# GNN and Mamba-2 kernel: weighted features stationary in the second adjacency round, Mamba stages three slots later

## The chip, the cores and the metric

The kernel runs on one core of a Trainium2 chip. The metric is the device time of one execution in microseconds (us). A core has five engines that run side by side and wait for each other by semaphores: TensorE (PE in the rows; its weight loads are PEld), VectorE (DVE), ScalarE (ACT), GpSimd (POOL) and SyncE (SP), which here only issues DMAs.

## The reference, cut to what matters

With N = 4096 rows and F = 128 features, a graph layer is followed by a Mamba-2 layer over the sequence of rows:

```
x = layernorm(x0)
U = softmax(where(adj > 0, leaky_relu(x@a1 + (x@a2).T), -9e15), axis=1)
rowsum = sum(U * 0.5 * U, axis=1)
feat = shrink(U@x, x, rowsum)              # round one over adj
pu = U @ feat                              # round two over adj
h = x0 + mix(feat, pu, rowsum, h0)         # = x1 in the kernel
out = h + mamba2(layernorm(h))             # chunks of 128 rows, state carried on
```

Since the leaky relu has two branches, exp(e) factors on each of them into a row weight times a column weight. So U @ v is two products of 0/1 masks with column-weighted features, `row0 * (maskA @ (w0*v)) + row1 * (maskC @ (w1*v))`, divided by the row's sum.

## The kernel before, in words

There are 32 row tiles of 128 rows (NT). Round one turns the adjacency into one byte per edge, `code` (0: no edge, 1 and 2: the two branches), four row tiles (a supertile, IT = 4) at a time, and multiplies the masks made of it with the features. SP writes ("spills") the codes to DRAM, one row tile of 4096 columns per DRAM row, for round two.

Round two runs in slots, one per row tile. In a slot four blocks of eight column tiles follow each other (NB = 4, JB = 8). Per block ScalarE makes maskA and VectorE maskC (128x1024 each, 4 buffers, made two blocks ahead), and `products` multiplies: per side eight matmuls, each with a 128x128 piece of the mask as the stationary operand and 256 columns of `Y` moving. `Y` holds the column-weighted features in two parts, high and low, which are two halves of a bank of the accumulator (accA or accC, two buffers each). Then ScalarE scales accA (`read_acc`, L1005), and VectorE joins accC, adds the halves and makes x1 (L792, L809, L814).

Between the blocks of slot s the Mamba stages of older tiles are worked off, as a software pipeline of five stages (`ok[0]` to `ok[4]`): x1, statistics and normalisation of tile s-1; projection and convolution of s-2 (VectorE's nine L842); decays and turned inputs of s-3; the chunk's outputs of s-4 (p_g, p_y, p_o); the output of tile s-4 (L805) and its store one slot later. GpSimd makes in each slot: rstd2 (L521, L522, after ln_done), x1b (L525), then `base_of` of the slot's own tile (L490 to L509), the decay matrix (L532), four products (L540 to L546) and rs_ready (L552, L553). All queues are in program order. The order within a slot is written out by hand on every engine. `schedule` writes the first 8 slots and the last 4 plus 5 draining ones out one by one, and puts the 20 between them into a hardware loop of four slots a turn.

On VectorE the slot is: gm (L785), the joined sums (L792), wmix (L799), mask(0), the output (L805, waits for rs_ready), x1 (L809, L814), mask(1), statistics (L827, L852), convolution with the small dt chain and the y sums between, yg (L934), mask(2), L940, L942, mask(3). The masks are L638 on VectorE and L986 on ScalarE.

Of the kernel before, what the change touches and what calls it, by code (L numbers as in the profile page):

```python
# [29 lines left out]
P = 128  # L30
# [6 lines left out]
def gnn_ffn_kernel(nc, x, adj, h0, a, temp, W_in, conv_w, conv_b, dt_bias, A_log, D, norm_w, W_out, W_lin, b_lin, out):  # L37
# [20 lines left out]
    with ExitStack() as ctx:  # L58
# [38 lines left out]
        acc_s = sb("acc_s", [P, 2, 2, XC])  # L97
        ps_sum = sb("ps_sum", [P, 2, 2, XC])
# [18 lines left out]
        class Space:  # L117
# [48 lines left out]
        base = adj_space.take(2, F)  # L166
# [22 lines left out]
        yT = adj_space.take(KB, P)  # L189
        state = code_space.take(2, DI)  # L190
# [3 lines left out]
        sum2 = y_space.take(2 * F)  # L194
# [14 lines left out]
            exp_done out_done zcopy""".split()  # L209
# [15 lines left out]

        def schedule(eng, slot):

            def fixed(s_):
                slot(s_, s_ % SLOTS, s_ < NT, s_ + 1 < NT, [0 <= s_ - d < NT for d in range(1, STAGES + 1)])

            for s_ in range(2 * SLOTS):
                fixed(s_)
            with eng.Fori(0, NT // SLOTS - 3) as u:
                for k in range(SLOTS):
                    slot(u * SLOTS + (k + 2 * SLOTS), k, True, True, [True] * STAGES)
            for s_ in range(NT - SLOTS, NT + STAGES):
                fixed(s_)

# [6 lines left out]
        def _(sp):  # L245
# [83 lines left out]
            def slot(s_, k, now, then, ok):  # L329
                if not isinstance(s_, int) or s_ + SLOTS - 1 < NT:  # L330
                    load_codes(s_ + (SLOTS - 1), (k + SLOTS - 1) % SLOTS)
                if then:
                    load_rows(s_ + 1, (k + 1) % 2)
                if ok[4]:
                    store(s_ - 5, (k - 1) % 2)
# [7 lines left out]
        def _(pool):  # L343
# [141 lines left out]
            def base_of(s_, k):  # L485
# [13 lines left out]
                link(g.tensor_tensor(w, wz, r, ALU.mult))  # L499
                link(g.tensor_tensor(wz, w, zn, ALU.mult))  # L500
# [8 lines left out]
                link(g.tensor_tensor(base[:, k % 2], featw[:, 0], featw[:, 1], ALU.add))  # L509
# [5 lines left out]
            def slot(s_, k, now, then, ok):  # L515
# [10 lines left out]
                if now:  # L526
                    base_of(s_, k)
# [33 lines left out]
        def _(dve):  # L561
# [169 lines left out]
            def mask2(n, k, j):  # L731
# [3 lines left out]
                mask_c(n + R1, code[:, 0, k, b * JB * P:(b + 1) * JB * P], b)  # L735

# [34 lines left out]
            def slot(s_, k, now, then, ok):  # L771
                def mask(j):

                    if (now and not (isinstance(s_, int) and s_ == 0) if j + LEAD < NB else then):
                        mask2(s_ * NB + (j + LEAD), (k + (j + LEAD) // NB) % SLOTS, j + LEAD)
# [3 lines left out]
                part = sum2.rearrange("p (a b) -> p a b", a=2)  # L779
# [6 lines left out]
                if ok[0]:  # L786

                    T = s_ - 1
                    row = v.snap(T) if not isinstance(T, int) else T
# [17 lines left out]
                if ok[0]:  # L807
                    dve.wait_ge(S["vch"], halves)
                    halves = step(v.tensor_tensor(part[:, 0], part[:, 0], part[:, 1], ALU.add))  # L809
                if ok[0]:  # L810

                    dve.wait_ge(S["vch"], halves)
# [552 lines left out]
```

## Time and profile before

| | |
|---|---|
| time, median of 3 runs (lowest, highest) | 981.47 us (979.46, 982.36) |
| span of the profiled execution | 981.8 us; no other time of that execution is given |
| TensorE, VectorE, ScalarE, GpSimd busy | 88%, 79%, 61%, 66% |
| mean granted TensorE clock | 0.926 of 2.4 GHz |
| round one / change of rounds / round two | to about 405 us / about 440 us / to the end |

The profile is one execution. A row of the timeline has the start and the duration in us, the engine, the line, the operation, output and inputs with their shapes, and how many of them are merged; in brackets stands the idle time of the engine before it and who ended it. A row of the groups (`--lines` of the trace) has the busy time in us and the mean duration in ns, then the idle time ahead. A row of the stretches gives for each engine the busy us and the count of instructions in the order PE, PEld, DVE, ACT, POOL, then the granted clock, the DMA engines' busy share and GB/s. Matmuls are pipelined: a single one's duration holds its latency, so the spacing of a run of them says more.

### The profile page before, as it was taken

How to read it: one execution, taken by the hardware profiler on the slowest of the kernel's cores; microseconds unless marked ns; L12 is line 12 of the kernel's file. 1: busy time of each engine (PE TensorE's matmuls, PEld its weight loads, DVE VectorE, ACT ScalarE, POOL GpSimd, SP SyncE). 2: the span in 40 equal slices, each digit the busy share in tenths (PEclk: the TensorE clock that was granted, in tenths of full speed). 3: DMA queues.
4: the chain of work that ended last, by engine and by line, in shares of the span. 5: the costliest groups of instructions: out<-in, count | busy, mean ns of one | idle time of the engine just before them, and what ended most of it. 6: DMA issues, size and time to landing. Idle time of an engine off the chain costs nothing.

```text
span 981.8 us, 22010 instructions
## 1 busy us (share of the span) xinstructions
PE 868.8 (88%) x6584; PEld 773.2 (79%) x6584; DVE 778.9 (79%) x2063; ACT 596.0 (61%) x1031; POOL 651.5 (66%) x1368
## 2 busy tenths in 40 slices
PE   4857999989989999649899898999899989999966
PEld 2647999989989999549788787878788877888844
DVE  6678899979988996576989787777777778688872
ACT  2358878868777786245666565555555655666541
POOL 5352566646664667886777777877777778777742
PEclk9768999999999999859999999999999998999975
DMA  6166977969778686001111111111111111100000
GB/s 174 53 203 185 302 260 226 311 190 294 256 237 270 197 284 208 1 22 55 55 39 58 35 56 38 50 34 51 36 51 37 51 37 51 37 30 17 3 7 9
DMA packets 97401, 110.72 MB, mean 113 GB/s; under 512 B 6320, under 2 KB 89136, under 8 KB 97328
## 3 DMA queue, kind: packets, MB, share of 16 engines
q1 hardware_dynamic: 97328, 109.75, 35.2%
q8 instruction: 46, 0.75, 0.3%
q14 instruction: 27, 0.22, 0.1%
HBM read 90.85 MB, written 18.87 MB: 112 GB/s over the span
## 4 chain that ended last, share of the span: by engine, by line
POOL 49%; issue 17%; PE 13%; DVE 12%; DMA 4%; ACT 3%; POOLq 1%; SPq 1%; DVEq 0%; ACTq 0%
POOL featw L505 6%; PE accA L1175 4%; PE accC L1182 4%; DMA adj_in<-in_adj_dram 3%; POOL f_rows L542 3%; POOL adj_in L540 3%; POOL adj_in L544 2%; DVE code L630 2%; PE ps L1165 2%; POOL featw L503 2%; POOL ywork L546 2%; ACT edges L981 2%; POOL adj_in L509 2%; POOL featw L508 2%; POOL f_rows L553 2%
## 5 line engine op out<-in xcount | busy, mean ns | idle before, releaser
L1175 PE MATMUL accA<-Y,maskA 128*128 128x260 f32 (+1 forms) x2048 | 322.1, 302 | 27.7 <-DVE Y L614 18.1
L1175 PEld LDWEIGHTS accA<-Y,maskA 128*128 128x128 f32 x2048 | 274.6, 198 | 46.7 <-issue 20.7
L986 ACT ACTIVATE maskA<-code 128x1024 fp32r<-128x1024 int8 x256 | 268.7, 1052 | 56.0 <-PE accC L1182 30.4
L1182 PE MATMUL accC<-Y,maskC 128*128 128x260 f32 (+1 forms) x2048 | 299.4, 290 | 1.4 <-DVE maskC L638 1.4
L1182 PEld LDWEIGHTS accC<-Y,maskC 128*128 128x128 f32 x2048 | 273.0, 197 | 1.9 <-DVE maskC L638 1.9
L638 DVE TENSOR_SCALAR maskC<-code 128x1024 fp32r<-128x1024 int8 x256 | 205.7, 808 | 0.0
L630 DVE SCALAR_TENSOR_TENSOR code<-f_rows,neg_f,ps 128x512 int8<-128x512 f32 x256 | 178.0, 738 | 25.9 <-PE ps L1165 24.5
L981 ACT ACTIVATE edges<-adj_in 128x1024 bf16<-128x1024 f32 x128 | 132.4, 1043 | 14.6 <-DMA adj_in<-in_adj_dram 14.4
L1165 PE MATMUL ps<-ident,edges 128*128 128x128 bf16 x1024 | 84.0, 227 | 19.0 <-ACT edges L981 12.3
L842 DVE SCALAR_TENSOR_TENSOR code<-adj_in,f_rows,code 128x128 f32<-128x128 f32 x288 | 94.8, 349 | 0.0
L1165 PEld LDWEIGHTS ps<-ident,edges 128*128 128x128 bf16 x1024 | 60.9, 101 | 29.6 <-ACT edges L981 10.2
L428 POOL COPY small<-roww 128x2 f32 (+1 forms) x32 | 6.4, 200 | 84.5 <-DVE ps_sum L656 82.8
L805 DVE SCALAR_TENSOR_TENSOR adj_in<-ps,f_rows,adj_in 128x128 f32<-128x128 f32 x32 | 11.2, 350 | 62.6 <-POOL f_rows L553 62.6
L521 POOL TENSOR_TENSOR f_rows<-f_rows,consts 128x1 f32<-128x1 f32 x32 | 8.4, 264 | 75.5 <-DVE f_rows L852 75.5
L505 POOL TENSOR_TENSOR featw<-featw,adj_in 128x128 f32<-128x128 f32 x32 | 56.8, 1774 | 2.5
L1285 PE MATMUL ps<-adj_in,code 128*128 128x64 f32 x256 | 35.1, 283 | 14.5 <-issue 12.2
L532 POOL TENSOR_TENSOR f_rows<-f_rows 128x512 f32<-128x512 f32 x32 | 34.4, 1076 | 18.9 <-DVE f_rows L924 11.4
L1086 ACT ACTIVATE f_rows<-f_rows 128x4 f32<-128x4 f32 x32 | 6.7, 208 | 66.3 <-DVE f_rows L887 66.3
L1072 ACT COPY code<-ps 128x260 f32<-128x260 f32 x32 | 12.0, 376 | 57.3 <-PE ps L1275 57.3
L1285 PEld LDWEIGHTS ps<-adj_in,code 128*128 128x128 f32 x256 | 32.7, 200 | 17.5 <-issue 14.7
L972 ACT CAST Y<-ywork 128x1040 fp32r<-128x1040 f32 (+1 forms) x16 | 16.7, 1052 | 42.3 <-DVE ywork L609 26.4
L1116 ACT COPY adj_in<-ps 128x256 f32<-128x256 f32 x32 | 12.0, 374 | 42.9 <-PE ps L1321 42.9
(187 smaller groups left out, 1622.2 us busy)
## 6 DMA issues: line engine op xcount, KB each, us to landing
adj_in<-in_adj_dram SPq DMA_DIRECT2D x128, 512.0 KB, 4.8
edge_codes<-code SPq DMA_DIRECT2D x8, 2048.0 KB, 9.7
code<-edge_codes SPq DMA_DIRECT2D x32, 512.0 KB, 3.3
xn<-in_x_dram SPq DMA_DIRECT2D x4, 512.0 KB, 5.7
adj_in<-in_x_dram SPq DMA_DIRECT2D x32, 64.0 KB, 1.8
adj_in<-in_L_gnn_h_dram SPq DMA_DIRECT2D x32, 64.0 KB, 1.9
out_dram<-adj_in SPq DMA_DIRECT2D x32, 64.0 KB, 1.6
f_rows<-in_L_ffn_W_in_dram SPq DMA_DIRECT2D x1, 192.0 KB, 6.5
```

The costliest lines, as they stand in the source:

```text
L505: link(g.tensor_tensor(featw[:, 0], featw[:, 0], x_in[:, k % 2], ALU.add))
L532: g.tensor_tensor(dam, upto.unsqueeze(1).broadcast_to([P, NH, P]), tiny[:, 2 + k % 2, NH:2 * NH].unsqueeze(2).broadcast_to([P, NH, P]), AL ...
L540: link(g.tensor_tensor(heads(xdt, HD), heads(xl[:, 0:DI], HD), dtc.unsqueeze(2).broadcast_to([P, NH, HD]), ALU.mult))
L630: v.scalar_tensor_tensor(out=code[:, par, :, jt * P:(jt + 1) * P], in0=f1_rows[:, rows].rearrange("p (i r) -> p i r", i=IT), scalar=neg_f2 ...
L638: v.tensor_scalar(maskC[:, b % MASKS], src, 2.0, None, ALU.is_equal).then_inc(S["maskC_ready"], 1)
L842: ins = v.scalar_tensor_tensor(out=conv[:, cb], in0=hist[:, k2, cb, tap:tap + P], scalar=conv_wt[:, cb, tap:tap + 1], in1=conv[:, cb], op0 ...
L981: s.activation(edges[:, h % 4], adj_in[:, h % 4], ACT.Sign).then_inc(S["signed"], 1)
L986: s.activation(maskA[:, b % MASKS], src, ACT.Relu, bias=-2.0).then_inc(S["maskA_ready"], 1)
L1165: m = t_.matmul(ps[jt % TRB][:, it * P:(it + 1) * P], edges[:, b % 4, it, j * P:(j + 1) * P], ident2[:], start=True, stop=True)
L1175: t_.matmul(accA[k][:, 0:2 * cols], maskA[:, b % MASKS, l * P:(l + 1) * P], Y[:, jt, 0, :, 0:cols], start=jt == 0, stop=jt == NT - 1)
L1182: m = t_.matmul(accC[k][:, 0:2 * cols], maskC[:, b % MASKS, l * P:(l + 1) * P], Y[:, jt, 1, :, 0:cols], start=jt == 0, stop=jt == NT - 1)
L1285: t_.matmul(ps[0][:, h * HD:(h + 1) * HD], wmix[:, h], xdt[:, h * HD:(h + 1) * HD], start=True, stop=True)
```

## The change

In round two the operands of the matmuls change places. A 128x128 piece of `Y` (one column tile, one side, high or low) is stationary, and the masks of four row tiles, 512 columns, move. A slot of products (a step) now covers eight column tiles of a group of four row tiles, so a group takes four steps; all sums of a group, transposed, gather in one bank per side (accA[0], accC[0]). After the group's last step ScalarE copies accA[0] and VectorE accC[0] to `turned`, and for each row tile two transposes (`turn_sums`) bring the two sides into accA[1], from where VectorE makes x1 with two operations. GpSimd prepares the row weights (`rowsc`). The spill writes the codes so that a DRAM row holds eight column tiles of four row tiles, in runs of 1 KB. The Mamba stages, `base_of`, the row loads and the stores stand three slots later (BEHIND = 3), so there are 40 steps instead of 37; the first 12 and the last 12 are written out and 16 are in the hardware loop.

```diff
+        BEHIND = IT - 1
         def schedule(eng, slot):
             def fixed(s_):
-                slot(s_, s_ % SLOTS, s_ < NT, s_ + 1 < NT, [0 <= s_ - d < NT for d in range(1, STAGES + 1)])
+                m = s_ - BEHIND
+                slot(s_, s_ % SLOTS, s_ < NT, s_ + 1 < NT, s_ // SLOTS, m, m % SLOTS, 0 <= m < NT,
+                     [0 <= m - d < NT for d in range(1, STAGES + 1)])
-            for s_ in range(2 * SLOTS):
+            for s_ in range(3 * SLOTS):
                 fixed(s_)
-            with eng.Fori(0, NT // SLOTS - 3) as u:
+            with eng.Fori(0, NT // SLOTS - 4) as u:
...
+        def quarter(k, b):
+            part = code[:, 0, k, :].rearrange("p (i j) -> p i j", i=IT)[:, :, b * 2 * P:(b + 1) * 2 * P]
+            return part.rearrange("p i (t c) -> p t i c", t=2)
...
-                dst = code_dram[bass.ds(row, IT)].rearrange("i p j -> p i j")
-                sp.dma_start(dst, code[:, par]).then_inc(S["spilled"], 16)
+                dst = code_dram[bass.ds(row, IT)].rearrange("q p (i c) -> p i q c", i=IT)
+                sp.dma_start(dst, code[:, par].rearrange("p i (q c) -> p i q c", q=NB)).then_inc(S["spilled"], 16)
```

On GpSimd, in `base_of`:

```diff
                 link(g.tensor_tensor(w, wz, r, ALU.mult))
+                link(g.tensor_tensor(rowsc[:, k % 2], roww[:, bass.ds(row, 1), :].rearrange("p a b -> p (a b)"), w.broadcast_to([P, 2]), ALU.mult))
```

On VectorE (the mask, the copy of a group's sums, x1):

```diff
-                mask_c(n + R1, code[:, 0, k, b * JB * P:(b + 1) * JB * P], b)
+                wait(dve, "mm_done", n + (R1 - MASKS + 1))
+                v.tensor_scalar(mask_slot(maskC, b), quarter(k, b), 2.0, None, ALU.is_equal).then_inc(S["maskC_ready"], 1)
...
+                if kk == 0 and (not isinstance(grp, int) or 1 <= grp <= NG):
+                    dve.wait_ge(S["mm_done"], step_ * NB + R1)
+                    v.tensor_copy(turned[:, 1], accC[0][:, :]).then_inc(S["c_copied"], 1)
...
-                    dve.wait_ge(S["acc_read"], T + (NT + 1))
-                    dve.wait_ge(S["base_done"], T + 1)
-                    halves = step(v.scalar_tensor_tensor(
-                        out=part, in0=accC[kt][:, 0:2 * F].rearrange("p (a b) -> p a b", a=2),
-                        scalar=roww[:, bass.ds(row, 1), 1:2].rearrange("p a b -> p (a b)"), in1=acc_s[:, kt, :, 0:F], op0=ALU.mult, op1=ALU.add))
...
-                    halves = step(v.tensor_tensor(part[:, 0], part[:, 0], part[:, 1], ALU.add))
+                    dve.wait_ge(S["p_x1"], T + 1)
+                    dve.wait_ge(S["base_done"], T + 1)
+                    half = step(v.scalar_tensor_tensor(out=sum2, in0=accA[1][:, 0:F], scalar=rowsc[:, kt, 0:1], in1=base_x[:, kt],
+                                                       op0=ALU.mult, op1=ALU.add))
...
-                    v.scalar_tensor_tensor(out=x1[:, kt], in0=part[:, 0], scalar=small[:, 14 + kt:15 + kt], in1=base[:, kt],
+                    dve.wait_ge(S["vch"], half)
+                    v.scalar_tensor_tensor(out=x1[:, kt], in0=accA[1][:, F:2 * F], scalar=rowsc[:, kt, 1:2], in1=sum2,
                                            op0=ALU.mult, op1=ALU.add).then_inc(S["x1_done"], 1)
```

ScalarE's mask changes in the same way, and its `read_acc` of round two becomes a copy of accA[0] in every fourth step. On TensorE:

```diff
+            def products2(n, j0, b, between):
+                for side, mask, acc, ready in ((0, maskA, accA[0], "maskA_ready"), (1, maskC, accC[0], "maskC_ready")):
+                    if side == 1 and between is not None:
+                        between()
+                    pe.wait_ge(S[ready], n + 1)
+                    for t in range(2):
+                        for half in range(2):
+                            m = t_.matmul(acc[:, :], Y[:, j0 + t, side, half, 0:F], mask[:, b % MASKS, t * IT * P:(t + 1) * IT * P],
+                                          start=j0 + t + half == 0, stop=j0 + t == NT - 1 and half == 1)
+                m.then_inc(S["mm_done"], 1)
...
+                        if ch == 0 and kk == 0:
...
+                                pe.wait_ge(S["acc_read"], grp + NT)
+                                pe.wait_ge(S["c_copied"], grp)
+                        early = isinstance(step_, int) and step_ < SLOTS
                         if early and ch == 0:
+                            pe.wait_ge(S["y2_done"], 2 * step_ + 2)
+                        products2(step_ * NB + (R1 + ch), kk * JB + ch * 2, ch, between)
...
+                def turn_sums():
...
+                    wait(pe, "x1_done", T)
+                    for side in range(2):
+                        m = t_.transpose(accA[1][:, side * P:(side + 1) * P], turned[:, side, t * P:(t + 1) * P], ident[:])
+                    m.then_inc(S["p_x1"], 1)
...
+                if ok[0] and kk != 0:
+                    turn_sums()
                 block(0)
+                if ok[0] and kk == 0:
+                    turn_sums()
```

## Rows read from the trace of the kernel before

**Rows 1.** The page, busy time, share of the span and instructions.
```profile
PE 868.8 (88%) x6584; PEld 773.2 (79%) x6584; DVE 778.9 (79%) x2063; ACT 596.0 (61%) x1031; POOL 651.5 (66%) x1368
```

**Rows 2.** Stretches, the second round's middle.
```profile
680.00:780.00 100.00, 93.70 (x631) 80.27 (x630) 75.54 (x262) 57.77 (x136) 76.39 (x141) 0.95 0.14 46
```

**Rows 3.** Chain of waits, 700 to 760 us, shares by line.
```profile
by line: issue 20.5%; POOL featw L505 17.4%; POOL f_rows L542 5.8%; POOL adj_in L540 5.6%; POOL adj_in L544 4.6%; POOL ywork L546 4.5%; POOL f_rows L553 3.7%; POOL featw L503 3.3%; POOL adj_in L509 3.1%; POOL featw L508 2.7%; POOL featw L50
```

**Rows 4.** Waits, 500 to 880 us: total us, times, longest us.
```profile
POOL f_rows L521 <- DVE f_rows L852: 54.7, 23, 2.6
...
DVE adj_in L805 <- POOL f_rows L553: 48.3, 23, 2.5
```

**Rows 5.** Timeline of VectorE, from the output to mask(1) in one slot.
```profile
774.10 0.35 DVE L805 SCALAR_TENSOR_TENSOR adj_in<-ps,f_rows,adj_in 128x128 f32<-128x128 f32 x1 [2.43 <-POOL f_rows L553]
...
774.95 0.69 DVE L638 TENSOR_SCALAR maskC<-code 128x1024 fp32r<-128x1024 int8 x1
```

**Rows 6.** Timeline of GpSimd, L521: first, loop's first, after loop, last two.
```profile
449.42 0.19 POOL L521 TENSOR_TENSOR f_rows<-f_rows,consts 128x1 f32<-128x1 f32 x1 [2.93 <-DVE f_rows L852]
...
545.54 0.20 POOL L521 TENSOR_TENSOR f_rows<-f_rows,consts 128x1 f32<-128x1 f32 x1 [2.56 <-DVE f_rows L852]
...
875.80 0.28 POOL L521 TENSOR_TENSOR f_rows<-f_rows,consts 128x1 f32<-128x1 f32 x1 [2.27 <-DVE f_rows L852]
...
922.13 0.28 POOL L521 TENSOR_TENSOR f_rows<-f_rows,consts 128x1 f32<-128x1 f32 x1 [2.27 <-DVE f_rows L852]
...
936.14 0.28 POOL L521 TENSOR_TENSOR f_rows<-f_rows,consts 128x1 f32<-128x1 f32 x1 [2.04 <-DVE f_rows L852]
```

**Rows 7.** Timeline of GpSimd and VectorE, a loop slot and a written-out one.
```profile
765.20 2.60 POOL L505 TENSOR_TENSOR featw<-featw,adj_in 128x128 f32<-128x128 f32 x1
765.40 0.68 DVE L638 TENSOR_SCALAR maskC<-code 128x1024 fp32r<-128x1024 int8 x1
...
896.50 0.60 POOL L505 TENSOR_TENSOR featw<-featw,adj_in 128x128 f32<-128x128 f32 x1
896.70 0.95 DVE L638 TENSOR_SCALAR maskC<-code 128x1024 fp32r<-128x1024 int8 x1
...
897.18 0.73 POOL L508 TENSOR_TENSOR featw<-col_mean,small 128x128 f32<-128x128 f32 x1
```

**Rows 8.** Timeline of TensorE, runs of matmuls.
```profile
415.27 2.04 PE L1175 MATMUL accA<-Y,maskA 128*128 128x256 f32 x8 [8.49 <-DVE Y L614]
...
761.01 1.10 PE L1302 MATMUL ps<-f_rows 128*128 128x512 f32 x2
...
761.96 0.49 PE L1304 MATMUL ps<-ident,code 128*128 128x128 f32 x3
...
769.02 1.12 PE L1182 MATMUL accC<-Y,maskC 128*128 128x256 f32 x8
```

**Rows 9.** Groups of instructions by line and shape, whole span.
```profile
L1302 PE MATMUL ps<-f_rows 128*128 128x512 f32 x64 | 37.2, 663 | 0.0
...
L432 POOL TENSOR_TENSOR small<-small,q_c 128x2 f32<-128x2 f32 x32 | 15.8, 492 | 2.5
...
L614 DVE TENSOR_TENSOR Y<-ywork,Y 128x1024 fp32r<-128x1024 f32 x8 | 9.9, 1276 | 1.1 <-ACT Y L972 1.1
...
L809 DVE TENSOR_TENSOR ywork<-ywork 128x128 f32<-128x128 f32 x32 | 9.4, 294 | 0.0
...
L430 POOL TENSOR_TENSOR small<-acc_s,small 128x2 f32<-128x2 f32 x32 | 6.3, 197 | 2.6
...
L959 ACT COPY code<-accA 128x512 f32<-128x512 f32 x8 | 4.7, 588 | 10.2 <-PE accA L1136 10.2
```

**Rows 10.** DMA issues: count, KB each, median us to landing.
```profile
adj_in<-in_adj_dram SPq DMA_DIRECT2D x128, 512.0 KB, 4.8
edge_codes<-code SPq DMA_DIRECT2D x8, 2048.0 KB, 9.7
```

**Rows 11.** Timeline of TensorE, the features' mean between the rounds.
```profile
437.42 0.80 PE L1237 MATMUL ps<-featsum,ones 128*128 128x128 f32 x2 [0.42 <-POOLq L471]
```

More of the change, by code:

```diff
@@ L189, in gnn_ffn_kernel @@
         yT = adj_space.take(KB, P)
+        rowsc = adj_space.take(2, 2)
         state = code_space.take(2, DI)
@@ L193, in gnn_ffn_kernel @@
         junk = y_space.take(DI)
-        sum2 = y_space.take(2 * F)
+        sum2 = y_space.take(F)
         tiny = rows_space.take(16, 8)
@@ L327, in _, with slot @@
             load_rows(0, 0)
-            def slot(s_, k, now, then, ok):
+            def slot(s_, k, now, then, grp, m, km, base, ok):
                 if not isinstance(s_, int) or s_ + SLOTS - 1 < NT:
                     load_codes(s_ + (SLOTS - 1), (k + SLOTS - 1) % SLOTS)
-                if then:
-                    load_rows(s_ + 1, (k + 1) % 2)
+                if not isinstance(m, int) or 0 < m + 1 < NT:
+                    load_rows(m + 1, (km + 1) % 2)
                 if ok[4]:
-                    store(s_ - 5, (k - 1) % 2)
+                    store(m - 5, (km - 1) % 2)
             schedule(nc.sync, slot)
@@ L513, in heads, with slot @@
                 return ap.rearrange("p (h w) -> p h w", h=NH)
-            def slot(s_, k, now, then, ok):
+            def slot(step_, kk, now, then, grp, s_, k, base, ok):
                 if ok[0]:
@@ L769, in heads, with slot @@
                 return ap.rearrange("p (h w) -> p h w", h=NH)
-            def slot(s_, k, now, then, ok):
+            def slot(step_, kk, now, then, grp, s_, k, base, ok):
                 def mask(j):
-                    if (now and not (isinstance(s_, int) and s_ == 0) if j + LEAD < NB else then):
-                        mask2(s_ * NB + (j + LEAD), (k + (j + LEAD) // NB) % SLOTS, j + LEAD)
+                    if (now and not (isinstance(step_, int) and step_ == 0) if j + LEAD < NB else then):
+                        mask2(step_ * NB + (j + LEAD), (kk + (j + LEAD) // NB) % SLOTS, j + LEAD)
                 k2 = k % 2
                 kt = (k - 1) % 2
-                part = sum2.rearrange("p (a b) -> p a b", a=2)
+                if kk == 0 and (not isinstance(grp, int) or 1 <= grp <= NG):
+                    dve.wait_ge(S["mm_done"], step_ * NB + R1)
+                    v.tensor_copy(turned[:, 1], accC[0][:, :]).then_inc(S["c_copied"], 1)
                 if ok[4]:
@@ L1050, in _, with slot @@
             y_high(3, F, (("y2_prod", 6), ("y2_prod", 7)), "y2_hi")
-            def slot(s_, k, now, then, ok):
+            def slot(step_, kk, now, then, grp, s_, k, base, ok):
                 def mask(j):
-                    if (now and not (isinstance(s_, int) and s_ == 0) if j + LEAD < NB else then):
-                        mask2(s_ * NB + (j + LEAD), (k + (j + LEAD) // NB) % SLOTS, j + LEAD)
-                if ok[0]:
-                    read_acc(s_ - 1, (k - 1) % 2, F, 1)
+                    if (now and not (isinstance(step_, int) and step_ == 0) if j + LEAD < NB else then):
+                        mask2(step_ * NB + (j + LEAD), (kk + (j + LEAD) // NB) % SLOTS, j + LEAD)
+                if kk == 0 and (not isinstance(grp, int) or 1 <= grp <= NG):
+                    act.wait_ge(S["mm_done"], step_ * NB + R1)
+                    if isinstance(grp, int) and grp == 1:
+                        act.wait_ge(S["scaled_done"], NT)
+                    else:
+                        wait(act, "x1_done", step_ - IT)
+                    s.copy(turned[:, 0], accA[0][:, :]).then_inc(S["acc_read"], 1)
                 if ok[1]:
@@ L1166, in turn, with products @@
                     m.then_inc(S["tr_done"], 1)
-            def products(n, k, b, ch, cols, y=None, between=None):
+            def products(n, k, b, ch, cols, y=None):
                 pe.wait_ge(S["maskA_ready"], n + 1)
@@ L1176, in products @@
                               start=jt == 0, stop=jt == NT - 1)
-                if between is not None:
-                    between()
                 pe.wait_ge(S["maskC_ready"], n + 1)
```

75 lines of the change are left out of this document (40 added, 35 removed).

## The prediction

> **What bounds the kernel now.** I read the page's busy line first: TensorE 88%, VectorE 79%, GpSimd 66% [rows 1]. Then the stretches: the second round's middle (680 to 780 us) has TensorE busy 93.7 of 100 us at a granted clock of 0.95 and GpSimd only 76.4 [rows 2]. That looks TensorE-bound, but matmuls overlap, so I went on to the chain of waits between 700 and 760 us. There the reader is to see L505 (17.4%) and other GpSimd lines, and no matmul line [rows 3]. The waits from 500 to 880 us say the same: GpSimd waits 54.7 us for VectorE's L852, VectorE 48.3 us for GpSimd's L553 [rows 4].
>
> So one slot is a loop: GpSimd L521 (rstd2 of one tile), `base_of`, the products for two older tiles, L553 (rs_ready); then VectorE L805 (output), L809 and L814 (x1), mask(1), L827, L852; then GpSimd again. VectorE idled 2.43 us before L805 [rows 5]. The period is read at L521: 32 starts from 449.42 to 936.14 [rows 6]. The 20 periods of the hardware loop's slots (545.54 to 875.80) take 16.51 each, the three written-out ones after them (to 922.13) 15.44, and the last, free of masks, 14.01.
>
> Why do loop slots take 1.1 us more? In them GpSimd's L505 takes 2.60 us: it is issued just ahead of VectorE's mask(2) and finishes only after mask(2), L940, L942 and mask(3) are all through. In written-out slots the same instruction takes 0.60 and the mask gives way (0.95) [rows 7]. Nineteen of 20 loop slots show the first form and the eight full written-out slots the second, at nearly the same offsets (L505 0.20 us ahead of the mask in both).
>
> **The change, part by part.**
>
> *Products.* Before: 64 matmuls of 256 columns a slot, eight in 1.12 us with the last 0.28 long, so 0.120 apiece [rows 8]. 256 columns at 2.4 GHz are 0.107, so 0.013 is overhead. After: 32 matmuls of 512 columns. The trace has no single-pass one; the nearest row, L1302, has two double-pass ones in 1.10 us (first start to last end) with 0.663 for one [rows 8, 9], so 0.437 for 1,024 columns, overhead 0.010. I take 0.213 + 0.013 = 0.226; the bounds are 0.213 (no overhead) and 0.240 (twice 0.120, nothing gained). A slot: 7.68 to 7.23, saving 0.45 (0 to 0.86). Two transposes are added, 0.107 each by L1304 (three in 0.49, one some 0.27) [rows 8]. Net: 0.24 us less TensorE work a slot. VectorE's 2.43 us wait before L805 hides it: in a slot whose end GpSimd sets, it is worth 0.
>
> The Trainium skill (Perfetto Trace Analysis, Identifying the Most-Contended Engine) judges TensorE's headroom by its LDWEIGHTS busy share, 79% here as VectorE's [rows 1], and the change halves the loads of round two. By that rule TensorE sets the slot and the sum is that of the rival so named below; the chain of waits disagrees.
>
> *x1 on VectorE.* L792 and L809 (0.294 [rows 9]) go, and L814 becomes a second reader of PSUM. L792's wait for base_done moves behind L805. On the loop stood L805, L809, L814, mask(1): 774.10 to 774.95 [rows 5]. After: L805, a PSUM read like it (0.35), then the dependent one: 0.35 against 0.28 for L809, so +0.07 a slot (0 to +0.2). L799 and mask(0) no longer stand behind base_done; they lie in VectorE's wait, cost 0.
>
> *GpSimd.* `base_of` has one instruction more (`rowsc`, 128x2). The nearest rows are L430, 0.197, and L432, 0.492, of that shape [rows 9], plus 0.07 issue: +0.27 (0.2 to 0.56), on the loop. In a slot where L505 waits out the masks anyway, it is absorbed: L505 just starts later and ends at the same time. Elsewhere it is paid in full.
>
> *Copies.* Every fourth slot ScalarE and VectorE copy 512 columns out of PSUM (L959, 0.588 for such a copy [rows 9]) in place of four smaller L1005. Block 0 and behind it the queue of TensorE wait for both. ScalarE's copy follows mask(3) and ends some 0.6 us after TensorE would have started. Then the transposes come behind block 0 (1.8 us), 3 us after the slot's start, still ahead of L805. Cost 0; if the cover were gone, 1 us in each of 7 slots.
>
> *Spill.* Runs of 1 KB instead of 4 KB on SP's queue, in front of the next adjacency loads. The adjacency loads (1 KB runs) land 512 KB in 4.8 us, the spill 2,048 KB in 9.7 [rows 10]: per byte the runs of 1 KB take twice as long at most. I take +1 us (0 to +4) for round one. SP's row loads and stores shift with the Mamba stages and keep their order towards base_done.
>
> *The shift by three slots.* This is the large term. Before, tile 0's sums are ready after slot 0; after, only after step 3. Step 0 no longer needs the later quarters of Y, so its blocks run while Y is made, but block 3 stands behind `feature_mean` (0.80 from 437.42 [rows 11]) and starts at 438.2. At the lower clock here, 1.2 GHz (eight matmuls of 256 in 2.04 against 1.12 [rows 8]) it ends at 441.6. Then 12 blocks of eight: 96 x 0.226 = 21.7, +1.7 for the rest of the lower clock: 465.0. Copies 0.8, block 0 1.8, transposes 0.4, two x1 steps 0.7, mask(1) 0.7, statistics and handover 0.6: 470.0 for the first L521, against 449.42: **+20.6** (17 to 24). It stands on the masks keeping up: a block takes 1.81, VectorE's mask 0.68 [rows 7], and ScalarE's in parallel, hidden.
>
> *The 31 periods between first and last L521.* Before: 486.7. After, the hardware loop holds 16 slots instead of 20, and the last three tiles run with neither masks nor products. The seven periods ahead of the loop, 96.1 (449.42 to 545.54), become eight: 96.1 + 15.44 + 1.0 for the first three, which fill the pipeline, + 5 x 0.34 (0.07 and 0.27, above) = 114.3. The loop: 16 at 16.57 (16.51 without its one short slot) + 0.07 = 16.64: 266.2. Three written-out ones at 15.44 + 0.34 = 15.78: 47.3. Four mask-free at 14.01 + 0.34 = 14.35: 57.4. Sum 485.2: **-1.5**.
>
> *Tail.* From the last L521 (936.14) to the end the same stages run, with the clock a little lower for want of products: +1 (0 to +3).
>
> **Sum.** 981.8 + 20.6 - 1.5 + 1 + 1 = **1002.9**. The page gives the execution's span, 981.8; no time of that execution beside it is shown, and the median of the three runs is 981.5, so I add nothing.
>
> **Rivals.**
>
> *All masked slots locked* (1009.8). The later L505 falls inside mask(2) also in the written-out slots: 8 x (16.64 - 15.78) = 6.9 more. For: it is now 0.27 later against masks that stay. Against: all 8 written-out slots escaped before.
>
> *No slot locked* (989.1). The shifted L505 gets in between mask(2) and L940, as L508 did in the written-out slot (0.73) [rows 7]: 16 x 0.86 = 13.8 less. The Trainium skill (SBUF — State Buffer, on the shared port pair) says that a GpSimd and a contending VectorE instruction exclude each other for one whole instruction, whichever starts first; by this, one issued in the mask would wait for that mask only, and the time would be this rival's. The 2.60 us across four instructions does not agree.
>
> *VectorE's masks lose their fast form* (999). Source rows are now 128 bytes in a (2, 4, 128) pattern. At the rate of L614 (1.276 for 1,024 [rows 9]) each mask costs 0.6 more, one of them on the loop; if it then no longer held GpSimd, a loop slot would lose the 1.13 between 16.57 and 15.44. 16 slots at 16.1 and 8 at 16.4 make 389 in place of 392.4 (266.2 + 8 x 15.78).
>
> *TensorE sets the slot* (996): the net 0.24 us comes off 31 slots, 7 us (20 at the upper bound). For: its busy share. Against: its waits for VectorE and GpSimd stand in the chain, not theirs for it.
>
> *The copies and turned sums become the wait* (1010): x1 waits for p_x1 behind block 0, 1 us in 7 slots.
>
> *Faster* (966). GpSimd stops colliding with VectorE: L799 and mask(0), freed from base_done, fall outside GpSimd's products. The mask-free period, 14.01, shows what is to be had; at 14.8 with `rowsc`, 24 slots take 355 instead of 392.4, 37 us less. The fill of 21 us over 24 slots is 0.87 each, so it decides where the mean masked period falls from the forecast 16.35 below 15.48, with one GpSimd instruction more than in the 15.44 of the best masked slots of before. For: base_done did hold L792 for 0.60 us. Against: the collisions follow VectorE's total, hardly changed.
>
> **How the numbers follow.** Likeliest, the sum with the loop slots locked: 0.36. All locked 0.18, none locked 0.24, slow masks 0.04, TensorE 0.04, copies 0.06, faster 0.08. The range 984 to 1013 takes in all but the faster rival, and leaves out heaped upper or lower bounds. A measurement of this kernel can tell about 0.3%. Faster 0.10 (the faster rival, and a none-locked run with every term at its low end), within 0.3% 0.04 (a none-locked run with a cheap fill), slower 0.86.
>
> **What would show it.** First L521 near 470; L1175's successor in steps of about 7.2 us before that; periods 16.6 in loop slots and L505's duration there, 2.6 or under 1; about 14.4 in the last four; product matmuls 0.226 apart. The prediction is wrong if the first L521 comes before 465, if masked periods fall below 15.3, or if round one moves by over 4 us.

## The result, and the profile after

The changed kernel takes 989.28 us (median of 5, 987.91 to 992.51), the kernel before beside it 982.36 (median of 5). The ratios of this document leave out one execution of the kernel before here, at 1594 us, and one of ten in e2, at 990.7 us. The ratio is 1.0073, with a 95% interval of 1.0045 to 1.0102: slower, as forecast, by 0.7% where 2.2% was forecast. The profiled execution took 987.91 and has a span of 986.2. So 1.7 us lie outside a span, which the sum against before's span left out; spans are compared with spans below.

The line numbers move. GpSimd's L521 is now L539, L504 and L505 are L522 and L523, L553 is L571; VectorE's mask in round two is L754, L805 is L817, L852 is L866, L940 is L954; the products are L1210. First the starts of L539 on GpSimd's timeline, which answer to [rows 6]:

```profile
469.70 0.19 POOL L539 TENSOR_TENSOR f_rows<-f_rows,consts 128x1 f32<-128x1 f32 x1 [21.95 <-DVE f_rows L866]
...
582.14 0.20 POOL L539 TENSOR_TENSOR f_rows<-f_rows,consts 128x1 f32<-128x1 f32 x1 [2.59 <-DVE f_rows L866]
...
835.53 0.28 POOL L539 TENSOR_TENSOR f_rows<-f_rows,consts 128x1 f32<-128x1 f32 x1 [2.40 <-DVE f_rows L866]
...
882.79 0.28 POOL L539 TENSOR_TENSOR f_rows<-f_rows,consts 128x1 f32<-128x1 f32 x1 [2.40 <-DVE f_rows L866]
...
940.51 0.28 POOL L539 TENSOR_TENSOR f_rows<-f_rows,consts 128x1 f32<-128x1 f32 x1 [1.92 <-DVE f_rows L866]
```

The first comes 20.28 later than before. The 31 periods take 470.81 instead of 486.72. The whole difference of the spans follows from this: 981.8 + 20.3 (the first start, with round one's -0.1 in it) - 15.9 (periods) + 0.0 (tail: 45.7 from the last start to the end in both) = 986.2. Forecast and measured, stretch by stretch:

| stretch | forecast | measured |
|---|---|---|
| first L539 | 470.0 | 469.70 |
| 8 periods ahead of the loop | 114.3 | 112.44 |
| 16 loop slots | 266.2 (16.64 each) | 253.39 (15.84 each) |
| 3 written-out slots | 47.3 | 47.26 |
| 4 slots without masks | 57.4 | 57.72 |
| tail against before | +1 | +0.0 |
| round one against before | +1 | -0.1 |

One line is wrong by 12.8 us; the rest are within 2. GpSimd and VectorE in a loop slot, the place of [rows 7]:

```profile
729.75 0.60 POOL L522 TENSOR_TENSOR featw<-featw 128x128 f32<-128x128 f32 x1
729.94 0.95 DVE L754 TENSOR_SCALAR maskC<-code 128x1024 fp32r<-128x1024 int8 x1
...
730.42 0.79 POOL L523 TENSOR_TENSOR featw<-featw,adj_in 128x128 f32<-128x128 f32 x1
730.82 0.68 DVE L954 SCALAR_TENSOR_TENSOR f_rows<-ywork,code 128x256 f32<-128x256 f32 x1
```

No GpSimd instruction takes 2.60 us any more, in any slot. It is the mask that gives way (0.95), as in before's written-out slots, and the addition of `x_in` takes 0.79. The waits between 500 and 880 us are those of [rows 4]:

```profile
POOL f_rows L539 <- DVE f_rows L866: 57.2, 24, 2.9
DVE adj_in L817 <- POOL f_rows L571: 53.2, 23, 2.5
```

So the loop of the slot still runs through GpSimd and VectorE. TensorE in the stretch of [rows 2], then its runs of products in the fill and its first block after the copies:

```profile
680.00:780.00 100.00, 96.32 (x475) 70.83 (x474) 83.11 (x268) 58.66 (x137) 74.08 (x153) 0.98 0.14 46
```

```profile
415.19 2.05 PE L1210 MATMUL accA<-maskA,Y 128*128 128x512 f32 x4 [8.57 <-DVE Y L632]
...
437.67 2.05 PE L1210 MATMUL accA<-maskA,Y 128*128 128x512 f32 x4
...
441.23 1.91 PE L1210 MATMUL accA<-maskA,Y 128*128 128x512 f32 x4
...
445.94 1.09 PE L1210 MATMUL accA<-maskA,Y 128*128 128x512 f32 x4
...
462.65 1.09 PE L1210 MATMUL accA<-maskA,Y 128*128 128x512 f32 x4
...
463.58 1.10 PE L1210 MATMUL accC<-maskC,Y 128*128 128x512 f32 x4
...
464.72 0.58 ACT L1077 COPY sums<-accA 128x512 f32<-128x512 f32 x1 [2.60 <-PE accC L1210]
465.51 1.17 PE L1210 MATMUL accA<-maskA,Y 128*128 128x512 f32 x4 [0.83 <-ACT sums L1077]
467.44 0.38 PE L1303 MATMUL accA<-ident,sums 128*128 128x128 f32 x2
467.86 0.35 DVE L824 SCALAR_TENSOR_TENSOR ywork<-accA,adj_in 128x128 f32<-128x128 f32 x1 [1.85 <-PE accA L1303]
```

Here the whole fill is to be seen: the round's first block at 415.2, block 3 from 437.7, 12 more blocks from 441.2 to 464.7, the copies, block 0 from 465.5, the turned sums at 467.4 and x1 at 467.9. The nine blocks that start from 445.94 on, of eight matmuls each, take 16.71 us up to the start at 462.65. So the matmuls of 512 columns are 0.232 apart; 0.226 was taken, with 0.240 as its upper bound.

### The profile page after: what moved, and what is told of

Same layout as the page of the kernel before. It is cut to its first block, busy times and chain, and to the rows that moved or that the text cites. A ratio compares the mean times of both kernels' runs of the same rounds, so it can differ in the third digit from the quotient of the medians.

```text
span 986.2 us, 19925 instructions
## 1 busy us (share of the span) xinstructions
PE 871.2 (88%) x5624; PEld 711.7 (72%) x5624; DVE 783.9 (79%) x2039; ACT 587.3 (60%) x1007; POOL 635.4 (64%) x1400
## 4 chain that ended last, share of the span: by engine, by line
POOL 45%; PE 18%; issue 18%; DVE 11%; ACT 3%; DMA 3%; POOLq 1%; SPq 1%; DVEq 0%; ACTq 0%
PE accA L1193 4%; PE accC L1198 4%; POOL adj_in L558 3%; POOL f_rows L560 2%; DVE code L648 2%; POOL featw L519 2%; DMA adj_in<-in_adj_dram 2%; POOL featw L523 2%; PE accA L1210 2%; PE ps L1183 2%; PE accC L1210 2%; POOL adj_in L527 2%; POOL adj_in L562 2%; POOL featw L522 2%; POOL small L454 2%
## 5 line engine op out<-in xcount | busy, mean ns | idle before, releaser
L1210 PE MATMUL accA<-maskA,Y 128*128 128x512 f32 x512 | 156.3, 428 | 22.3 <-DVE Y L632 8.6
L1193 PE MATMUL accA<-Y,maskA 128*128 128x260 f32 x1024 | 156.0, 296 | 9.5 <-ACT maskA L1000 6.6
L1210 PE MATMUL accC<-maskC,Y 128*128 128x512 f32 x512 | 146.8, 410 | 0.0
L1198 PE MATMUL accC<-Y,maskC 128*128 128x260 f32 x1024 | 145.8, 286 | 1.1 <-DVE maskC L656 1.1
L1193 PEld LDWEIGHTS accA<-Y,maskA 128*128 128x128 f32 x1024 | 133.6, 193 | 10.0 <-ACT maskA L1000 6.9
L1049 ACT ACTIVATE maskA<-code 128x1024 fp32r<-128x1024 int8 x128 | 133.8, 1049 | 10.1 <-PE accC L1210 9.9
L1198 PEld LDWEIGHTS accC<-Y,maskC 128*128 128x128 f32 x1024 | 133.3, 192 | 1.3 <-DVE maskC L656 1.3
L1210 PEld LDWEIGHTS accA<-maskA,Y 128*128 128x128 f32 x512 | 90.8, 195 | 53.2 <-issue 27.9
L754 DVE TENSOR_SCALAR maskC<-code 128x1024 fp32r<-128x1024 int8 x128 | 111.6, 876 | 11.0 <-PE accC L1210 10.9
L1210 PEld LDWEIGHTS accC<-maskC,Y 128*128 128x128 f32 x512 | 97.9, 195 | 22.4 <-DVE maskC L754 0.9
L656 DVE TENSOR_SCALAR maskC<-code 128x1024 fp32r<-128x1024 int8 x128 | 97.3, 766 | 0.0
L817 DVE SCALAR_TENSOR_TENSOR adj_in<-ps,f_rows,adj_in 128x128 f32<-128x128 f32 x32 | 11.2, 351 | 72.8 <-POOL f_rows L571 72.8
L539 POOL TENSOR_TENSOR f_rows<-f_rows,consts 128x1 f32<-128x1 f32 x32 | 8.5, 266 | 92.7 <-DVE f_rows L866 92.7
L550 POOL TENSOR_TENSOR f_rows<-f_rows 128x512 f32<-128x512 f32 x32 | 37.6, 1176 | 19.0 <-PE ps L1356 8.2
## 6 DMA issues: line engine op xcount, KB each, us to landing
edge_codes<-code SPq DMA_DIRECT2D x8, 2048.0 KB, 10.2
```

The source lines that it names most:

```text
L550: g.tensor_tensor(dam, upto.unsqueeze(1).broadcast_to([P, NH, P]), tiny[:, 2 + k % 2, NH:2 * NH].unsqueeze(2).broadcast_to([P, NH, P]), AL ...
L656: v.tensor_scalar(maskC[:, b % MASKS], src, 2.0, None, ALU.is_equal).then_inc(S["maskC_ready"], 1)
L754: v.tensor_scalar(mask_slot(maskC, b), quarter(k, b), 2.0, None, ALU.is_equal).then_inc(S["maskC_ready"], 1)
L1049: s.activation(mask_slot(maskA, b), quarter(k, b), ACT.Relu, bias=-2.0).then_inc(S["maskA_ready"], 1)
L1193: t_.matmul(accA[k][:, 0:2 * cols], maskA[:, b % MASKS, l * P:(l + 1) * P], Y[:, jt, 0, :, 0:cols], start=jt == 0, stop=jt == NT - 1)
L1198: m = t_.matmul(accC[k][:, 0:2 * cols], maskC[:, b % MASKS, l * P:(l + 1) * P], Y[:, jt, 1, :, 0:cols], start=jt == 0, stop=jt == NT - 1)
```

## The experiments

The question is why the loop slots are no longer locked out. A slot is called locked where one small GpSimd instruction takes 2.3 us or more beside mask(2) and mask(3). All ratios are to the kernel before on the same chip in the same session; its median was 982.4 beside the changed kernel, 977.3 beside e1 to e4, 979.0 beside e5 to e7, 983.7 beside e8 and e9, and 986.6 beside e10 to e12. So times of different sessions are not to be subtracted. The period and the locked slots are those of one profiled execution for each kernel; in e2, e4 and e11 it was the fastest of its kernel's, in e7 the slowest.

| run | ratio (95%) | us | loop period | locked in loop |
|---|---|---|---|---|
| kernel before (first profile) | | 981.5 | 16.51 | 19 of 20 |
| changed kernel | 1.0073 (1.0045 to 1.0102) | 989.3 | 15.84 | 0 of 16 |
| e1_extra_at_rowsc | 0.9949 (0.9929 to 0.9969) | 972.0 | 15.74 | 0 of 20 |
| e2_extra_at_end | 1.0073 (1.0037 to 1.0110) | 981.6 | 16.22 | 9 of 20 |
| e3_w_behind_L505 | 1.0230 (1.0178 to 1.0282) | 998.2 | 16.71 | 19 of 20 |
| e4_after_rowsc_at_end | 1.0209 (1.0162 to 1.0256) | 996.3 | 16.30 | 8 of 16 |
| e5_before_swapped_adds | 0.9993 (0.9968 to 1.0019) | 977.8 | 16.09 | 11 of 20 |
| e6_after_swapped_adds | 1.0114 (1.0091 to 1.0137) | 989.6 | 15.84 | 0 of 16 |
| e7_after_no_low_half | 1.0003 (0.9980 to 1.0026) | 979.5 | 15.82 | 0 of 16 |
| e8_before_027_earlier | 0.9873 (0.9857 to 0.9890) | 971.1 | 15.52 | 0 of 20 |
| e9_before_two_extra | 1.0033 (1.0017 to 1.0048) | 987.5 | 16.29 | 0 of 20 |
| e10_before_best | 0.9805 (0.9778 to 0.9831) | 968.3 | 15.62 | 1 of 20 |
| e11_after_best | 1.0074 (1.0055 to 1.0093) | 994.3 | 16.22 | 4 of 16 |
| e12_before_again | | 984.2 | 16.51 | 19 of 20 |

### One instruction, at two places

```diff
                 link(g.tensor_tensor(w, wz, r, ALU.mult))
+                link(g.tensor_tensor(rowsc[:, k % 2], roww[...], w.broadcast_to([P, 2]), ALU.mult))
                 link(g.tensor_tensor(wz, w, zn, ALU.mult))
```

> The kernel before with one GpSimd instruction more: rowsc (128x2) is computed where the change computes it, between w and wz*zn in base_of, and nobody reads it. Theory 1 (the lock-out of L505 ended because the added GpSimd instruction moves L505 off the moment 0.2 us ahead of VectorE's mask(2)): L505 takes 0.6 to 0.8 us in the loop slots instead of 2.60, the 20 loop periods fall from 16.51 to about 15.8 (15.44 of the written-out slots plus 0.27, and a little for the slot in four that runs longer), and the time falls by 20 x 0.7 - 12 x 0.27 = 11 us, to about 971. Theory 2 (the lock-out ended because of what the change does on VectorE and TensorE): L505 still takes 2.3 to 2.6 us in the loop slots, absorbs the 0.27, the loop periods stay at 16.5, and the time is 982 to 985.

The periods are 15.74 and no slot is locked, as theory 1 had it: a kernel that does more work than before and is 0.5% faster. Its time, 971.98, is theory 1's as a number, but here the kernel before took 977.3, so the gain is 5.3 us where 11 were expected. Whether the kernel before had fewer than 19 locked slots on this chip is not known, as it was not profiled there. The slot looks like that of the changed kernel:

```profile
600.79 0.59 POOL L506 TENSOR_TENSOR featw<-featw 128x128 f32<-128x128 f32 x1
600.99 0.95 DVE L640 TENSOR_SCALAR maskC<-code 128x1024 fp32r<-128x1024 int8 x1
...
601.47 0.79 POOL L507 TENSOR_TENSOR featw<-featw,adj_in 128x128 f32<-128x128 f32 x1
```

The same instruction behind the last line of `base_of`:

> The kernel before with the same added instruction, but at the end of base_of, behind L505 and L509, so that L505 starts as before relative to L521. Theory 1: the lock-out stays (L505 at 2.60 in the loop slots) and every slot pays 0.27 more: loop periods 16.5 to 16.8, time 982 to 990, so some 11 to 19 us more than the same instruction costs at its own place. Theory 2: the same here, 982 to 990, and the run at the other place gives the same time as this one.

It costs 9.6 us more here than at rowsc's place by the medians and 12 by the ratios; 11 to 19 were expected. The lock-out stays, but in 9 of 20 loop slots only, in an execution 6 us below the run's median. GpSimd and VectorE in one free and one locked loop slot of this run:

```profile
727.48 0.61 POOL L504 TENSOR_TENSOR featw<-adj_in,coef 128x128 f32<-128x128 f32 x1
727.74 0.36 DVE L923 SCALAR_TENSOR_TENSOR f_rows<-f_rows 128x4 f32<-128x4 f32 x1
...
728.70 0.60 POOL L506 TENSOR_TENSOR featw<-featw,adj_in 128x128 f32<-128x128 f32 x1
728.90 0.95 DVE L640 TENSOR_SCALAR maskC<-code 128x1024 fp32r<-128x1024 int8 x1
...
805.31 0.64 POOL L504 TENSOR_TENSOR featw<-adj_in,coef 128x128 f32<-128x128 f32 x1
805.58 0.39 DVE L923 SCALAR_TENSOR_TENSOR f_rows<-f_rows 128x4 f32<-128x4 f32 x1
...
806.59 2.60 POOL L506 TENSOR_TENSOR featw<-featw,adj_in 128x128 f32<-128x128 f32 x1
806.79 0.68 DVE L640 TENSOR_SCALAR maskC<-code 128x1024 fp32r<-128x1024 int8 x1
```

L506 stands 0.20 us ahead of the mask in both. The two slots differ already where GpSimd's L504 and VectorE's L923 meet: 0.61 and 0.36 in the free one, 0.64 and 0.39 in the locked one.

This small difference tells the slots apart in every profile in which the last of the two additions stands there (the kernel before twice, e2, e4, e5, e10). Of their full slots with masks, all 69 in which that addition was locked have VectorE's instruction (L921 in the kernel before) at 0.38 to 0.40, and of the 89 free ones 86 have it at 0.35 or 0.36. The other three, at 0.39 and free, are the loop's second slot in the kernel before, its second profile and e5. So what an addition meets at the mask shows about 1 us ahead of it. This is a reading of the profiles; no run changed that meeting alone.

The reverse in the changed kernel, with rowsc moved behind the sum into `base_x`:

> The changed kernel with rowsc moved to the end of base_of, so that the x_in addition (L505 of the kernel before) starts about 0.27 us earlier, where it stood in the kernel before relative to the first instruction of the slot. Theory 1: the lock-out comes back in the 16 loop slots (2 us or more in one instruction), loop periods rise from 15.84 to 16.5, time about 989 + 11 = 1000. Theory 2 (VectorE's new order ended it): the addition stays at 0.6 to 0.8, periods at 15.8, time 987 to 990.

The time is 996.32. The changed kernel was not timed beside it; by the ratios (1.0209 against 1.0073) the run is 13 us above it. 8 of 16 loop slots are locked (L522 at 2.60 in seven, its successor at 2.54 in one). So the changed kernel can be locked out too, and rowsc's place is what keeps it free. The rival, that VectorE's new order ended it, is out; so is the exact form of theory 1, by which all 16 should be locked.

### Earlier, later, exchanged

Both edits below move lines of `base_of` behind the addition of `x_in`; e3 moves all three lines, e8 only the last.

```diff
-                wait(pool, "x1_done", s_ - 1)
-                link(g.tensor_tensor(w, wz, r, ALU.mult))
-                link(g.tensor_tensor(wz, w, zn, ALU.mult))
...
                 link(g.tensor_tensor(featw[:, 0], featw[:, 0], x_in[:, k % 2], ALU.add))
+                wait(pool, "x1_done", s_ - 1)
+                link(g.tensor_tensor(w, wz, r, ALU.mult))
+                link(g.tensor_tensor(wz, w, zn, ALU.mult))
```

> The kernel before without any added instruction: L499 and L500 (w and wz*zn) and their wait for x1_done are moved behind L505, so L505 is issued some 0.5 us earlier, at a time at which VectorE is still at other work, and the total of GpSimd's work is the same. Theory 1: L505 takes 0.6 to 0.8 in all slots, loop periods fall from 16.51 to 15.44 to 15.6, the time by 18 to 21 us, to about 962. Theory 2 (L505 meets the masks in any case, or another GpSimd instruction gets locked out in its place): one instruction of base_of still takes 2 us or more in the loop slots, periods stay at 16.3 to 16.6, time 978 to 984.

It is 2.3% slower, 21 us, which neither theory had; theory 2 gave 978 to 984. The addition of `x_in` escapes (0.46), and `w`, a single element per partition, is caught in its place in 19 of 20 loop slots and in every full written-out one:

```profile
791.12 2.33 POOL L505 TENSOR_TENSOR small<-small 128x1 f32<-128x1 f32 x1
791.32 0.68 DVE L639 TENSOR_SCALAR maskC<-code 128x1024 fp32r<-128x1024 int8 x1
```

So the size of the instruction does not matter. Its identity might:

> The kernel before with the last two additions of base_of's first half exchanged: featw += x_in comes first, featw += coef*h0 second. No instruction is added, and each stands at the other's time. In the run with the dead instruction and in the changed kernel an addition of featw's two halves stood exactly 0.20 us ahead of mask(2), where L505 stood, and it was never locked out. Theory A (which GpSimd instruction stands there decides: the one that reads x_in gets locked out, the one that adds featw's halves does not): no slot is locked, loop periods 15.44 to 15.6, some 14 to 18 us below the kernel before on this chip. Theory B (only the moments decide, whatever the instruction; the added instruction helped because everything ahead of it came 0.1 us otherwise): as many slots are locked as in the kernel before, periods 16.5, time within 4 us of the kernel before.

> The changed kernel with the same two additions exchanged, so that the addition of x_in now stands 0.20 us ahead of mask(2). Theory A: the lock-out appears in the changed kernel (2 us or more in that addition in a third to all of the loop slots), 4 to 14 us above the changed kernel's 989. Theory B: it stays away, periods 15.84, time 987 to 991.

The exchange changes nothing in the times: the kernel before is still locked (11 of 20, ratio 0.9993), the changed kernel still free (15.84, 989.58 us). Theory A is out. Theory B stands, except for its number of locked slots: periods of 16.5 were expected and 16.09 came.

> The kernel before with only L500 (wz*zn, 0.19 and its issue) moved behind L505, so that the three instructions ahead of L505 and L505 itself come 0.27 us earlier; no instruction is added. So far L505's group 0.54 earlier was locked out in 26 of 27 masked slots, in its own place in 9 to 19 of 20 loop slots, 0.27 later in none. Theory C (a narrow bad place near the old one; each shift of 0.27 may miss it, and the run at 0.54 earlier met another): no or few locked slots, loop periods 15.4 to 15.6, time 12 to 18 us below the kernel before. Theory D (whatever GpSimd issues in the 0.2 us ahead of mask(2) is at risk in all kernels in which it comes no later than before): locked in at least half of the loop slots, periods 16.0 to 16.6, time from 4 below to 5 above the kernel before.

The periods of the loop are 15.52, none is locked, and the ratio is 0.9873: theory C. The timeline shows why "earlier" is the wrong word, in one loop slot and in one written-out slot:

```profile
601.32 0.60 POOL L504 TENSOR_TENSOR featw<-featw,adj_in 128x128 f32<-128x128 f32 x1
601.52 0.95 DVE L638 TENSOR_SCALAR maskC<-code 128x1024 fp32r<-128x1024 int8 x1
...
865.40 2.33 POOL L505 TENSOR_TENSOR small<-small 128x1 f32<-128x1 f32 x1
865.60 0.68 DVE L638 TENSOR_SCALAR maskC<-code 128x1024 fp32r<-128x1024 int8 x1
```

In the loop slot L502 had taken 0.88, the gain of 0.27 was lost in it, and the addition stands 0.20 ahead of the mask again, unharmed. In every full written-out slot `wz*zn` stands there and is locked out. In each of these kernels, then, some instruction is issued 0.20 ahead of mask(2), locked or not. It looks as if the two engines' earlier collisions bring them back into that order; no run tried this by itself.

> The kernel before with two dead 128x2 instructions at rowsc's place, so that everything behind comes 0.54 us later. If only coming later matters, no slot is locked, and it costs 0.27 a slot more than the run with one: periods 15.9 to 16.1, time 8 us above that run, so 1 to 4 us above the kernel before. If the free place is narrow, some instruction is locked out again in most loop slots: periods 16.6 to 17.1, time 12 to 20 above the kernel before.

No slot is locked; but the second dead instruction costs 0.55 a slot (16.29 against 15.74), not 0.27. Neither forecast of the periods (15.9 to 16.1, 16.6 to 17.1) came true, and the run is 0.3% above the kernel before, at the upper end of what was expected.

### Does TensorE set the slot?

```diff
-                        for half in range(2):
+                        for half in range(1):
```

> The changed kernel with half of the product matmuls of the second round left out: those of the low half of Y (its sums lack the small correction). If GpSimd and VectorE set the masked slot, as the sum took it, the periods of the loop stay at 15.7 to 15.9, and only the fill gets shorter: its 12 blocks go from 1.93 us each to the pace of ScalarE's mask (1.05 to 1.1), 10 us less, first L521's successor at about 460, time about 979. If TensorE sets the slot (3.7 us less work in each), the periods fall below 15.3 and the time below 970.

The stretch of the changed kernel's 96.32, with half of the products left out:

```profile
680.00:780.00 100.00, 79.21 (x362) 54.13 (x363) 80.90 (x262) 56.90 (x133) 72.77 (x150) 0.91 0.13 44
```

TensorE's busy time falls by 17 us in 100, and the loop period from 15.84 to 15.82. A TensorE busy for 96% of a stretch was not its bound. By the Trainium skill (Perfetto Trace Analysis, Identifying the Most-Contended Engine) TensorE's headroom is judged by MFU and its LDWEIGHTS busy share, not by its matmul busy share. The trace agrees: in the changed kernel's stretch the loads were busy for 71%, less than VectorE with 83%, and when they fell to 54% the time of a slot did not follow.

The first L539 comes at 462.80, 6.9 us earlier. But in this execution round one, which the edit does not touch, ended 3.0 us later: the second round's first block starts at 418.20, where it starts at 415.19 in the changed kernel. From there on it is 44.6 us to L539 instead of 54.5, so the fill got shorter by 9.9, as expected. The medians of e6 and e7, on one chip, differ by 10.1. The pace of the blocks was not the expected one:

```profile
418.20 1.19 PE L1210 MATMUL accA<-maskA,Y 128*128 128x512 f32 x2 [8.57 <-DVE Y L632]
...
448.12 0.87 DVE L754 TENSOR_SCALAR maskC<-code 128x1024 fp32r<-128x1024 int8 x1 [0.68 <-PE accC L1210]
...
449.83 0.69 DVE L754 TENSOR_SCALAR maskC<-code 128x1024 fp32r<-128x1024 int8 x1 [0.84 <-PE accC L1210]
...
454.18 0.69 DVE L754 TENSOR_SCALAR maskC<-code 128x1024 fp32r<-128x1024 int8 x1 [0.23 <-PE accC L1210]
...
455.11 0.70 DVE L754 TENSOR_SCALAR maskC<-code 128x1024 fp32r<-128x1024 int8 x1 [0.23 <-PE accC L1210]
```

Each mask waits for the block that frees its buffer, so the masks show the blocks' pace: 1.71 us apart at 448, 0.93 at 454. The granted clock of the stretch 442 to 462 is 0.77, against 0.96 in the changed kernel. The blocks at 0.93 also show that ScalarE's mask did not hold them at 1.05, as was expected.

### A version that beats both

```diff
+                late = not isinstance(s_, int)
+                if not late:
                     link(g.tensor_tensor(wz, w, zn, ALU.mult))
...
                 link(g.tensor_tensor(featw[:, 0], featw[:, 0], x_in[:, k % 2], ALU.add))
+                if late:
+                    link(g.tensor_tensor(wz, w, zn, ALU.mult))
```

> A version meant to beat both kernels: L500 stands behind L505 in the hardware loop's slots, where the profile of the run at 0.27 earlier showed no lock-out, and at its own place in the written-out slots, where the kernel before showed none. If both places are free together: 31 periods without a lock-out, loop periods 15.5, written-out 15.44, 7 slots times 0.8 = 5.5 us below the run with L500 late everywhere (971.1 on a chip where the kernel before took 983.7), so a ratio to the kernel before of 0.980 to 0.984. If what a slot meets is set by the slots ahead of it (the written-out ones only escaped because of their own past), some slots are locked out again and the ratio is 0.986 to 0.990.

The ratio is 0.9805, at the good end: 18 us below the kernel before, by moving one instruction in the hardware loop's slots. Two slots of the profile are still locked (the loop's third, and the last masked one). The same edit in the changed kernel, with rowsc at the end:

> The changed kernel with rowsc at the end of base_of and wz*zn behind the addition of x_in in the loop's slots. If the free place of the kernel before is free here too, its loop periods are 15.55 to 15.65 instead of 15.84, and the time is 983 to 986; the fill of 20 us stays, so it remains slower than the kernel before (ratio 1.001 to 1.005 where that takes 982). If it is not free, periods are 16.2 to 16.6 and the time is 993 to 998.

It fails, as the second of its forecasts had it (16.2 to 16.6, 993 to 998 us): 16.22 a slot, with the moved `wz*zn` at 2.33 in every fourth loop slot, and the others at 15.98 to 16.18 against 15.55 written out.

> The kernel before once more, unchanged, to see in a second profile how many of its 20 loop slots are locked out: 19 were in the profile at 981.8. If the number is a matter of each execution, its span should follow at 1.1 us a locked slot; if it is fixed by the code, it is 19 again and the span within 1 us of 981.8.

19 of 20 again, with the free one in the same place (the loop's second slot), the span at 982.5, and two written-out slots locked where the first profile had none. So two profiles agree on the loop and not on the slots ahead of it. That the number is the same in all executions is not shown: both profiles have long spans (981.8 and 982.5), and in e1's session the kernel before took from 971.26 to 980.65 us. At 1.1 us a locked slot this spread would be some eight of them, an estimate; part of it can be round one, which moved by 3.0 us in e7's profile.

## Why the prediction was off

**The step that failed** is the term "The loop: 16 at 16.57 + 0.07 = 16.64: 266.2", and in it the statement on `rowsc` that "in a slot where L505 waits out the masks anyway, it is absorbed". It took the lock-out for a property of the slot. Measured: 15.84 a slot, 253.4 in all, 12.8 us of the 16.7 by which the span was missed. The one dead instruction of e1 at that place takes the kernel before from 16.51 to 15.74 a slot, e4 shows the reverse in the changed kernel. So the added GpSimd work was no cost of 0.27 absorbed in a stall of 2; it removed the stall, and paid about half of the fill back (16 x 0.67 = 10.7 us). So in the kernel before experiments show that the instruction's place decides (e1 against e2); in the changed kernel e4 shows it for half of the loop slots.

**The rival "no slot locked"**, with 989.1 and 0.24, is what happened, with its mechanism (GpSimd gets in between mask(2) and its successor) on the timeline. That its number is so close to the time of 989.28 is luck: it is a span, and the measured span is 986.2, 2.9 less, most of it the tail and the spill at 1 us each and the 1.9 us ahead of the loop, against 0.9 more in the loop. The profile had spoken for the rival: at the same 0.20 us, 19 slots were locked and the written-out ones were not. Of these it has seven and not eight, four ahead of the loop and three behind it; the changed kernel has eight. The rows of the kernel before show the difference ahead of it, L921 at 0.39 in the loop and at 0.35 written out. So the result turns on a few hundredths of a microsecond, and a change that adds an instruction ahead of it draws again; the forecast still carried the old outcome over.

**The fill** was right: 470.0 forecast, 469.70 measured, by the steps named (block 3 from 437.7 against 438.2, 12 more blocks to 464.7 against 465.0). The direction rests on it.

**Ahead of the loop** 112.4 for 114.3: with slots at 15.75, as forecast (15.78), but the first three shorter by 0.35 to 0.54 than before's, where 1.0 more was added for the three together; the fourth, at 16.41, gave some back. Written-out and mask-free slots came within 0.3 us. **Tail and spill** were charged 1 us each and cost nothing: the spill lands in 10.2 us instead of 9.7, hidden in round one.

**TensorE** saved work and gained nothing, as the sum had it; e7 settles the rival. Of the products 0.25 us a slot was saved and not 0.45 (32 x 0.232 against 64 x 0.120), about what the two transposes add. **VectorE's masks** kept their fast form (0.68 where unimpeded). **The copies** did not become the wait: the slot in which they fall is 16.02 to 16.03, 0.15 above the next longest, and e1, which has no copies, has one of 15.90 in four as well. What is left between e1's 15.74 and the changed kernel's 15.84 is of the size of the x1 chain's +0.07; it was not tried alone. That the fill belongs to the shift is read from the timeline; the shift alone was not run.

**Open**: what decides whether an instruction that stands 0.20 us ahead of the mask is locked out. Its size (e3), its operands (e5) and its offset from the mask (e2, e8) do not. The meeting with L921 about 1 us earlier goes with the outcome in 155 of 158 slots, but why 0.03 us there lead to 2.60 at the mask was not found. Moving mask(2) on VectorE, the other side of the collision, was not tried.

## What to carry to other kernels

A stall that two engines make between them belongs to an exact order of instructions, not to a stage: price a change that adds an instruction ahead of it with the stall and without, and give both near equal chances when the profile shows both forms. Where such stalls show (one small instruction at several times its usual length), try to move one independent instruction first: here that was worth 2%, more than the rebuild of the second round cost or won. And before TensorE's work is cut, take half of it away and look at the period: at 96% busy it did not set the slot here. Where two profiles are compared, count from an event behind the part that the edit leaves alone: in e7 round one's 3.0 us would otherwise be taken for the fill's.

## What the hardware showed that was not expected

A GpSimd instruction was held for 2.33 (128x1) or 2.60 us (128x128) while four instructions of VectorE went through. The Trainium skill (SBUF — State Buffer, on the port pair that VectorE and GpSimd share) lets the one wait for one whole instruction of the other; the rows do not agree, the longest of those four being 0.68. In free slots the same 128x128 instruction takes 0.60 and the mask 0.95.

With half of the products left out, TensorE's granted clock in the fill (442 to 462 us) fell from 0.96 to 0.77, and in the middle of the round from 0.98 to 0.91. Over the whole span it was 0.867 to 0.885 in all ten executions, against 0.917 to 0.930 in the changed kernel's five. At the lower of the two levels (1.2 GHz) a block took 1.71, at the higher (2.4) 0.93. The three blocks from 446.1 to 451.1 went at the lower level, which is 2.2 us more than at the higher; ahead of them TensorE had waited 0.68 and 0.51 us for masks. In the changed kernel, without such waits, it was at the higher level from 444 on. So cutting TensorE's work cost it part of its clock.
